# Graph layers on one core: one product for the last source rows of two relations

## What is computed

```python
xb = h.reshape(N, B, S)                                      # 8 blocks of 12 channels
transformed = jnp.einsum('nbi,rbio->rnbo', xb, weights[l]).reshape(R, N, D)
msg = transformed[etype, src] * edge_norm                    # R = 8 relations
agg = jax.ops.segment_sum(msg, dst, num_segments=N)
h_new = agg + h @ loop_w[l] + bias[l]
h = jax.nn.relu(h_new) if l < L - 1 else h_new
```

## Time and profile before

| | |
|---|---|
| median of 3 runs (lowest, highest) | 2582.21 us (2578.12, 2589.15) |
| the profiled execution's own time | 2571.02 us |
| its span, first to last instruction | 2569.3 us |
| mean granted TensorE clock | 0.957 of full speed |
| PE busy | 2173.7 us (85%) |
| DVE busy | 2047.2 us (80%) |
| ACT busy | 1038.6 us (40%) |
| POOL busy | 709.7 us (28%) |
| the relational layers' products | 1619 to 1981 us and 2035 to 2395 us |

### The profile page before, as it was taken

One profiled execution on the slowest core, in us unless ns is written; L12 is line 12 of the kernel. 1 busy time (PEld: TensorE's weight loads), 2 busy tenths in 40 slices (PEclk: granted clock), 3 DMA queues, 4 the chain that ended last, 5 costly groups with the idle time before them and its releaser, 6 DMA issues. The chain is left out here.

```text
span 2569.3 us, 63293 instructions
## 1 busy us (share of the span) xinstructions
PE 2173.7 (85%) x22329; PEld 1800.9 (70%) x22330; DVE 2047.2 (80%) x3355; ACT 1038.6 (40%) x2085; POOL 709.7 (28%) x1336
## 2 busy tenths in 40 slices
PE   3788778799999998676777767899998999999897
PEld 2777777699999998211111213799898599989787
DVE  8888888765555664799999996799888699888546
ACT  1666666432333332699999995100000400000223
POOL 3655555200000000100000001466663266666000
PEclk8999999899999999799999997999999999999899
DMA  2333333211000100511111114332223423223610
GB/s 77 132 150 150 145 129 150 110 40 41 28 27 32 35 27 8 137 41 41 42 42 42 41 38 156 106 85 72 80 74 58 175 71 85 72 71 58 248 79 20
DMA packets 95191, 206.49 MB, mean 80 GB/s; under 512 B 21620, under 2 KB 61172, under 8 KB 94880
## 3 DMA queue, kind: packets, MB, share of 16 engines
q1 hardware_dynamic: 80544, 182.39, 20.3%
q0 software_dynamic: 14464, 21.44, 4.5%
HBM read 118.17 MB, written 84.76 MB: 79 GB/s over the span
## 5 line engine op out<-in xcount | busy, mean ns | idle before, releaser
L1816 PE MATMUL l_bank<-tab,mask 128*128 128x192 f16 x7600 | 653.5, 247 | 38.9 <-issue 30.0
L1816 PEld LDWEIGHTS l_bank<-tab,mask 128*128 128x128 f16 x7600 | 628.8, 98 | 59.7 <-issue 58.2
L1404 DVE TENSOR_SCALAR mask<-code 128x1600 int32<-128x1600 int32 x304 | 538.3, 1812 | 78.6 <-remote 39.0
L1788 POOL DMA_INDIRECT ggot<-table_dram,gidx x432 | 411.6, 953 | 240.9 <-issue 84.0
L1287 DVE SCALAR_TENSOR_TENSOR pr<-ex,cring 128x1568 f32<-128x1568 f32 x200 | 356.6, 1784 | 10.0 <-DMA cring<-c_dram 10.0
L1233 PE MATMUL att_acc<-pr,v 128*32 128x392 f32 x1600 | 184.8, 535 | 146.9 <-DVE pr L1287 138.1
L836 PE MATMUL sums<-onehots,ct 128*128 128x192 f16 x3125 | 263.6, 247 | 10.4 <-DVE onehots L902 6.3
L836 PEld LDWEIGHTS sums<-onehots,ct 128*128 128x128 f16 x3125 | 260.5, 98 | 13.4 <-issue 6.9
L836 PE MATMUL sums<-u,ct 128*128 128x192 f16 x3125 | 259.1, 246 | 0.0
L836 PEld LDWEIGHTS sums<-u,ct 128*128 128x128 f16 x3125 | 258.0, 98 | 0.0
L1261 ACT ACTIVATE ex<-score_rest,poss 128x1176 f32<-128x1176 f32 x200 | 248.7, 1244 | 2.8 <-PE score_rest L1225 2.6
(11 more groups left out here) (342 smaller groups left out, 3188.9 us busy)
## 6 DMA issues: line engine op xcount, KB each, us to landing
code<-code_dram SPq DMA_DIRECT2D x38, 800.0 KB
code_dram<-flat SPq DMA_DIRECT2D x100, 200.0 KB, 1.9
ct_dram<-ct SPq DMA_DIRECT2D x25, 800.0 KB, 4.0
c_dram<-flat SPq DMA_DIRECT2D x25, 800.0 KB, 3.4
ct_again<-ct_dram SPq DMA_DIRECT2D x25, 800.0 KB, 17.5
cring<-c_dram SPq DMA_DIRECT2D x200, 98.0 KB, 1.9
table_dram<-tab SPq DMA_DIRECT2D x50, 384.0 KB, 2.3
flat<-code_dram SPq DMA_DIRECT2D x19, 800.0 KB, 4.3
```

The costliest lines, as they stand in the source:

```text
L1404: e.tensor_scalar(turned.rearrange("p (s q d) -> p s q d", q=NQ, d=DQ // 2), words.rearrange("p (q s d) -> p s q d", q=NQ, d=DQ // 2), abs ...
L1788: e.indirect_dma_start(ggot[:, k, j, :], None, table_dram[:, :], bass.IndirectOffsetOnAxis(ap=gidx[:, k, j:j + 1], axis=0)).then_inc(s_ggo ...
L1816: mm = e.matmul(acc[k][:, 0:2 * D], mask[:, r % MR, s, :], tab[:, s, r, :], start=(r == 0 and s == 0), stop=(r == R - 1 and s == NT - 1))
```

## The change

It makes use of the padding of the last source tile. Its 53 rows fit into half of the partitions, so the rows of an odd relation are put into the partitions 64 to 127 beside those of the even relation ahead of it, in the table and in the code alike. One product then sums both, and the odd relations need 24 products, and masks of 24 tiles.

- `doubled_table` (new, DVE, once for each layer): copies rows 0 to 63 of tile 24 of `tab` for the four odd relations onto rows 64 to 127 of the even ones. It stands after the last `low_out`. SP's store of tile 24 waits for it (`s_paired`), and so does PE's first product.
- `doubled_rows` (new, DVE, once for each code tile): writes the code words of tile 24 of partitions 0 to 63, shifted right by 2 bits (that is by one relation), to partitions 64 to 127. 64 words for each partition. For code tile 0 it stands ahead of the first mask, for t + 1 behind mask 6 of tile t, with a wait there for the load of t + 1.
- `relation_mask`: odd relations take 24 tiles, 1536 words; r = 0 waits for `s_twice`.
- PE's loop: `NT - r % 2` products.

```diff
+                def doubled_rows(e, t):
+                    last = lambda p0: code[p0:p0 + HP, t % SLOTS, :, NT - 1, :].bitcast(I32)
+                    e.tensor_scalar(last(HP), last(0), 2, None, ALU.logical_shift_right).then_inc(s_twice, 1)
+
                 def relation_mask(e, t, r):
                     up = 10 - 2 * r
-                    turned = mask[:, r % MR, :, :].rearrange("p s d -> p (s d)").bitcast(I32)
-                    words = code[:, t % SLOTS, :, :, :].rearrange("p q s d -> p (q s d)").bitcast(I32)
+                    tiles_of = NT - r % 2
+                    if r == 0:
+                        e.wait_ge(s_twice, t + 1)
+                    turned = mask[:, r % MR, 0:tiles_of, :].rearrange("p s d -> p (s d)").bitcast(I32)
+                    words = code[:, t % SLOTS, :, 0:tiles_of, :].bitcast(I32)
                     e.tensor_scalar(turned.rearrange("p (s q d) -> p s q d", q=NQ, d=DQ // 2),
-                                    words.rearrange("p (q s d) -> p s q d", q=NQ, d=DQ // 2), abs(up), 0x0C000C00,
+                                    words.rearrange("p q s d -> p s q d"), abs(up), 0x0C000C00,
...
+                def doubled_table(e):
+                    e.wait_ge(s_lo, NT)
+                    of = lambda p0, first: tab[p0:p0 + HP, NT - 1, :, :].rearrange("p (r k) d -> p r k d", k=2)[:, :, first, :]
+                    e.tensor_copy(of(HP, 0), of(0, 1)).then_inc(s_paired, 1)
...
                                     e.wait_ge(s_lo, t + 1)
+                                    if t == NT - 1:
+                                        e.wait_ge(s_paired, 1)
                                     store_table(e, t)
...
                                     e.wait_ge(s_mask, t * R + (r + 1))
-                                    for s in range(NT):
+                                    if t == 0 and r == 0:
+                                        e.wait_ge(s_paired, 1)
+                                    for s in range(NT - r % 2):
                                         mm = e.matmul(acc[k][:, 0:2 * D], mask[:, r % MR, s, :], tab[:, s, r, :],
-                                                      start=(r == 0 and s == 0), stop=(r == R - 1 and s == NT - 1))
+                                                      start=(r == 0 and s == 0), stop=(r == R - 1 and s == NT - 2))
...
+                                    if r == MR + 2 and t + 1 < TD:
+                                        e.wait_ge(s_in[(t + 1) % SLOTS], 16 * ((t + 1) // SLOTS + 1))
+                                        doubled_rows(e, t + 1)
```

More of the change, by code:

```diff
@@ L1393, in gnn_kernel @@
                 s_mask = sem(nm + "mask")
+                s_twice, s_paired = sem(nm + "twice"), sem(nm + "paired")
+                assert N - (NT - 1) * P <= HP and R % 2 == 0
                 def load_code(e, t):
@@ L1595, in _ @@
                                 e.wait_ge(s_in[0], 16)
+                                doubled_rows(e, 0)
                                 for r in range(MR):
@@ L1598, in _ @@
                                     lows(13 + 3 * r, 16 + 3 * r)
+                                doubled_table(e)
                             @block.scalar
```

## The result

The changed kernel takes **2590.22 us** (median of 10 runs, 2585.86 to 2597.69) beside 2582.68 (10 runs, 2577.03 to 2589.15) of the kernel before: ratio **1.0031, interval 1.0017 to 1.0045**. The forecast was 2567.2 in 2554 to 2580, 15 us faster; it is 7.5 us slower. The profiled execution took 2585.86 us with a span of 2584.2.

A forecast was written before the change was run, and what follows sets the result against it. PE was taken as the bound, DVE following by four mask buffers; products -12.5, tile 1 -2.2, table stage -1.5, added copies +0.25 and +0.9 summed to -15.0 us from 2582.2, forecast 2567.2, range 2554 to 2580.

The forecast's parts named there:

- The products: Mask products on PE: 152 fewer over two layers at 82.5 ns each, -12.5 us.
- The odd masks: DVE's masks of odd relations: 24 tiles, even counts on both sides, so fast, 950 ns in place of 1812.
- the strides: Rival on DVE: strided reads keep odd masks slow at 1740 ns, -10.6 us in sum, 2571.6 us; chance 0.15.
- Tile 1: Tile 1 of each layer, where DVE is late: faster masks remove nearly all of two PE gaps, -2.2 us for both layers.
- Table stage: Layer 1's table stage: faster masks between `low_out` calls remove two of three ACT gaps, -1.5 us.
- Added work: New DVE copies: `doubled_rows` 0.2 us each, +0.25 before layer 0's first mask; `doubled_table` 0.35 plus wait, +0.9 for both layers.
- sum of -15.0: Whole kernel: -12.5 - 2.2 - 1.5 + 0.25 + 0.9 us, giving 2567.2 us.
- The 0.95 us between them: PE per tile: 18.44 us measured less 17.49 at full pitch, put down to two mid-product pauses of unknown cause.
- point (c): All tiles but tile 1: faster odd masks only lengthen DVE's waits for PE, 0 us.
- rival of worse pauses: PE in early tiles: shifted engine phase gives them the late tiles' pause rate, +10 us, 2577 us; chance 0.13.
- the 77 us: DVE's waits before masks for PE's products, taken as evidence that PE is the bound and DVE is not.
- POOL starved: Rival: fast masks stretch gathers, 4.4 us per tile, POOL falls behind, +57 us, 2624 us; chance 0.04.

The follow-up runs named there:

- before_traced: The kernel before, unchanged, run again on another chip to have its trace there; 2522.59 us.
- after_again: The changed kernel, unchanged, run again in a later group; 2509.68 us beside 2522.34 of the kernel before, ratio 0.9949.
- after: The changed kernel as first measured against the kernel before; 2590.22 us, ratio 1.0031.
- slow_odd: The changed kernel with odd masks of 25 tiles again (slow rate), still 24 products; 2570.90 us, 1.0003 of the kernel before.
- fast_alone: The kernel before with odd relations' masks made in two pieces, 24 tiles and 1, and all 25 products; 2577.14 us, ratio 1.0024.
- slow_odd_again: slow_odd, unchanged, run again in a later group; 2516.09 us, 0.9971 of the kernel before.
- short_odd: slow_odd with odd masks of only 13 tiles (832 words, slow rate) from tile 1 on; 2569.84 us, 0.9999 of the kernel before.
- slow_pool_by_mask: slow_odd with POOL's gathers paced by DVE's mask count in place of PE's product count; 2510.92 us, 0.9955 of the kernel before.
- six_spread: The kernel before with every second gather left out, six for each group, released one by one; 2517.74 us.
- one_gather_after: The changed kernel with one gather for each group in place of 12; 2507.14 us, 63 below the kernel before.

## Why the prediction was wrong

**The products**: right in size, 82.5 ns pitch, 7448 of them. Where PE doesn't pause, tiles go from 17.49 to 17.16 us, the 4 x 82.5 ns of the sum. **The odd masks**: 972 ns, 950 forecast; the parity of the outermost counts decided, not the strides. In the Trainium skill ("VectorE: DVE Perf Modes", What auto-detection actually checks) that is the rule, and 24 tiles bear it out as 25 did. **Tile 1**: in before_traced tiles 1 and 2 take 18.93 and 18.57 us (layer 0), in after_again 18.59 and 17.16, so 1.75 less, 0.66 of them the products: 1.1 for layer 0 and 0.9 for layer 1, 2.0 against the 2.2 of the sum. (A tile is taken here from last mask product to last mask product.) **Table stage**: two of three gaps gone, as forecast; around its second mask the calls of `low_out` start 1.80 and 1.10 us apart where they had 2.66, 0.93, 0.92 and 2.04, 0.75 us less for each. In the whole time between the two product stages, which is 51 to 54 us in the profiles whatever the kernel, the 1.5 can't be told. **Added work** in after, groups by line:

```profile
L1404 DVE TENSOR_SCALAR code<-code 64x64 int32<-64x64 int32 x38 | 7.7, 202 | 1.2
L1423 DVE COPY tab<-tab 64x768 f16<-64x768 f16 x2 | 0.8, 410 | 0.1
```

`doubled_rows` 202 ns (0.2 forecast), `doubled_table` 410 (350); from the last `low_out`'s end to PE's first product it is 1.97 us in layer 1 where it was 1.35, +0.6 against +0.45.

So the sum of -15.0 stands in the second condition: -12.7 and -16.2 were measured. **The step that failed** is the one by which the pauses were a constant: "The 0.95 us between them are two pauses in the middle of a product's 25 matmuls", "What makes these pauses the trace doesn't tell", and then point (c), faster masks in all other tiles "only lengthen DVE's waits: 0". They are not PE's alone. In the first condition they come with the gathers: fewer products only lengthen them, and the fast masks, which stretch the gathers, add more. The medians give the sizes. The forecast missed by 22.5 us (+7.5 against -15.0). slow_odd, for which the sum has -10.6, took +1.0: 11.6. fast_alone, for which tile 1 and the table stage alone were put at -3, took +7.2: 10.2. Together 21.8. The rival of worse pauses had +10 us at 0.13; it was those 22.5, or 29.9 between the two profiles, and its reason (the phase of the engines) was half of the matter: it went by the rates that before's own tiles showed, as if what the change made could not lie beyond them. (It also took the late tiles for some 308 us; nine tiles of 19.2 in two layers are 346.)

The trace of before did tell. Each pause in the earlier trace rows has a gather's end 0.8 us ahead of it and a gather's start 0.36 behind, and the 39.0 us of "remote" in the earlier trace rows are signals that came late, longest 4.5 us. I took "remote" for products of PE, and read PE's "issue" without asking what the other engines did at that moment. Mask by mask, 62 of the 77 us that DVE waited were time after the signal was due (0.28 us after the start of the product's last matmul); in after it is 145 us, in before_traced 0.4 of 28. So the 77 us were not room that DVE had, as the prediction used them: PE was the bound, but DVE followed much closer, as slow_odd_again shows.

**POOL starved** was priced too narrowly: I asked only whether gathers arrive late for PE. They never did, in any run. Their stretch was as large as thought: 145 ns for each of 12, 1.7 us in a tile, 0.44 for each fast mask. The Trainium skill ("SBUF — State Buffer", SBUF: two separate sides) has VectorE's fast modes locking GpSimd out while it writes descriptors; 1098 ns beside fast masks and 953 beside masks at the slow rate, also where these are as short (short_odd), agree. The stretch falls on the gathers that a fast mask meets: in after 136 of 432 overlap one and take 1406 ns in the mean, the others 957. Where it led in the first condition, to a third engine, the runs alone show.

**Open**: what makes the two conditions. The program, the chip, the granted clock (1.00 in the stretches shown, in both), the length of a gather and that of an instruction fetch (1071 and 1072 ns) are the same; which core of the chip ran, and where in memory the tables lay, is not on record. That PE's signals are held up during gathers in one and not in the other is shown; by what is not. Nor is it settled whether the number of gathers in a row or their sum sets the pauses (the runs meant for it met the other condition). In the profiles the two parts of the change, +10.9 us over the pitch for slow_odd and +5.0 for fast_alone, fall short of the +29.9; since their medians do add up, I put that down to single profiles, which is not shown.

## What to carry to other kernels

Idle time of the bounding engine that nothing ends ("issue", in the middle of a loop) is no constant of that engine: lay its ends against what all other engines begin and end there, before a sum is built on it. A change that speeds up an engine which isn't the bound can slow the bound by way of a third: look at whose instructions get longer beside it, here the gathers, 953 to 1098 ns. And a result of half a per cent holds for the condition it was measured in; the time of the kernel before, 2521 to 2524 or 2570 to 2583, says which one that is, so note it beside every ratio. Of the kernels that can be used, the changed one (2508 to 2510) and slow_pool_by_mask (2511) are level where PE doesn't pause, and none that was run where it does beats before there.

## What the hardware showed that I had not expected

- The same program on the same chip took 2569.92 us (23 runs) in one group and 2523.90 (7 runs) in another, with alike mean granted clocks (0.951 to 0.965 and 0.954 to 0.965 by run). The 46 us are mid-product pauses of PE: 54.9 against 6.8 in the profiles of before and before_traced.
- In the first condition, PE's signals reach DVE and POOL up to 4.5 us late (4.8 in after) while POOL issues gathers one behind another, and PE itself pauses some 20 matmuls after such a signal. In the second they take 0.28 us in the median and 0.36 at most, beside 12 gathers in a row.
- Gathers were stretched by 145 ns in the mean by fast masks of 1536 words, in both conditions. Those that overlapped a fast mask took 1406 ns in after and 1370 in after_again, the others 957 and 975.
- A gather that stands alone is no slower for it: in six_spread they took 958 ns. The 1295 ns of one_gather_after come from the fast masks too: the 21 of 36 that overlapped one took 1523, the others 976.
